# The causal mask moves from a matmul to the operation that finds each head's maximum

## The reference

```
h   = layernorm(x)
q   = rope(h @ Wq)        # 32 heads of 64
k   = rope(h @ Wk)        # 8 key-value heads of 64, each shared by 4 query heads
v   = h @ Wv
s   = q @ k.T / sqrt(64)
s   = where(key <= query, s, -3.4e38)         # the causal mask
out = softmax(s) @ v
x   = x + out @ Wo
x   = x + ffn(layernorm(x))   # activations rounded to int8 per token, int8 weights
```

## Time and profile before

| | before |
|---|---|
| median of 3 runs | 802.25 us (799.59 to 802.53) |
| profiled execution | span 803.9 us (the page gives no other time of it) |
| TensorE, weight loads | 761.0 us (95%), 640.0 us (80%) busy |
| VectorE, ScalarE, GpSimd | 629.2 us (78%), 628.4 us (78%), 569.1 us (71%) busy |
| granted TensorE clock, mean | 0.987 of full speed |
| mask matmuls (L720) | 352, mean 254 ns |
| maxima (L1367) | 352 reduces, mean 635 ns |
| exponentials (L1028) | 512, mean 530 ns, and 512 accumulator reads |

### The profile page before, as it was taken

How to read it: one execution, slowest core, us unless ns; L and a number is a source line. 1 busy time by engine, 2 the same in 40 slices (tenths; PEclk the granted TensorE clock), 3 DMA queues, 4 the chain that set the end, 5 groups by cost and what they waited for, 6 DMA issues and landing times.

```text
span 803.9 us, 23412 instructions
## 1 busy us (share of the span) xinstructions
PE 761.0 (95%) x8230; PEld 640.0 (80%) x8230; DVE 629.2 (78%) x1392; ACT 628.4 (78%) x1734; POOL 569.1 (71%) x524
## 2 busy tenths in 40 slices
PE   5799999999999999999999999999999999999993
PEld 3578888888888887788888888888888888888782
DVE  5757787777787887777788888887788877877887
ACT  4577888787877887787788778887788778888873
POOL 3467868787768786877786887778686787686402
PEclk9899999999999999999999999999999999999996
DMA  8255544554555554455554455455454555454300
GB/s 267 56 119 114 130 119 118 132 141 111 127 121 108 118 118 93 117 117 119 115 121 108 113 128 120 104 128 122 106 117 107 122 116 126 93 116 97 87 8 27
DMA packets 56994, 90.99 MB, mean 113 GB/s; under 512 B 12592, under 2 KB 19248, under 8 KB 56880
## 3 DMA queue, kind: packets, MB, share of 16 engines
q1 hardware_dynamic: 53808, 79.02, 43.0%
q0 software_dynamic: 3072, 10.49, 5.0%
HBM read 16.06 MB, written 2.10 MB: 23 GB/s over the span
## 4 chain that ended last, share of the span: by engine, by line
PE 71%; DVE 6%; ACT 6%; SPq 5%; issue 5%; DMA 5%; POOL 2%; ACTq 0%; POOLq 0%; DVEq 0%
PE x_bank L621 21%; PE t_bank L733 14%; PE o_bank L749 11%; PE s_bank L717 9%; PE s_bank L718 8%; DMA qT<-wv 4%; PE s_bank L720 3%; PE t_bank L621 3%; PE ot_bank L800 2%; ACT prob L1028 2%; SPq L303 2%; DVE probT L1356 2%; SPq L337 1%; SPq L341 1%; DVE o_norm L1391 1%
## 5 line engine op out<-in xcount | busy, mean ns | idle before, releaser
L1028 ACT ACTIVATE prob<-s_bank,neg_max 128x384 f32<-128x384 f32 (+3 forms) x512 | 266.1, 530 | 64.9 <-DVE neg_max L1367 64.8
L1367 DVE TENSOR_REDUCE neg_max<-s_bank 128x1 f32<-128x384 f32 (+3 forms) x352 | 215.6, 635 | 60.3 <-PE s_bank L720 57.3
L1356 DVE SCALAR_TENSOR_TENSOR probT<-t_bank,probT 128x512 f16<-128x512 f32 x320 | 215.4, 681 | 29.6 <-ACT probT L1040 28.8
L1040 ACT ACTIVATE probT<-t_bank 128x512 f16<-128x512 f32 x320 | 189.0, 600 | 43.8 <-PE t_bank L733 38.8
L733 PE MATMUL t_bank<-ident,prob 128*128 128x128 f32 x1280 | 199.1, 278 | 5.1 <-DVE probT L1356 1.7
L717 PE MATMUL s_bank<-kT,qT 128*128 128x384 f32 (+3 forms) x512 | 178.3, 363 | 6.7 <-DMA qT<-wv 4.2
L491 POOL TENSOR_TENSOR wv<-raw,wv 128x512 fp32r<-128x512 f32 x62 | 79.4, 1280 | 134.2 <-ACT wv L989 134.2
L718 PE MATMUL s_bank<-kT,qT 128*128 128x384 f32 (+3 forms) x512 | 157.1, 322 | 0.0
L733 PEld LDWEIGHTS t_bank<-ident,prob 128*128 128x128 f32 x1280 | 137.6, 141 | 15.0 <-issue 7.5
L749 PE MATMUL o_bank<-value,probT 128*128 128x64 f16 x3840 | 138.5, 193 | 0.0
L749 PEld LDWEIGHTS o_bank<-value,probT 128*128 128x128 f16 x3840 | 131.4, 98 | 6.1
(11 more groups left out here) (123 smaller groups left out, 946.8 us busy)
## 6 DMA issues: line engine op xcount, KB each, us to landing
qT<-wv SPq DMA_DIRECT2D x248, 128.0 KB, 2.4
swp<-raw SPq DMA_DIRECT2D x320, 64.0 KB, 2.0
kT<-key_pair SPq DMA_DIRECT2D x128, 128.0 KB, 2.4
wg_raw<-in_w_group POOLq DMA_DIRECT2D x16, 384.0 KB, 4.9
wg_raw<-in_w_group POOLq DMA_DIRECT2D x16, 256.0 KB, 4.3
resid<-in_x SPq DMA_DIRECT2D x4, 512.0 KB, 7.5
out<-resid SPq DMA_DIRECT2D x16, 128.0 KB, 2.1
wo_stage<-in_w_out SPq DMA_DIRECT2D x4, 256.0 KB, 3.5
```

Source lines behind the costliest of these rows:

```text
L1028: nc.scalar.activation(prob[:, slot:slot + blocks, h, :], s_bank[G % SCORE_BANKS][:, at * n:(at + 1) * n].rearrange("p (k n) -> p k n", n= ...
L1040: nc.scalar.activation(turned_half[B % TURNED][HI], t_bank[B % TURN_BANKS][:, :], ACT.Copy, scale=PROB_SCALE).then_inc(probT_hi, 1)
L1356: nc.vector.scalar_tensor_tensor(out=turned_half[B % TURNED][LO], in0=t_bank[B % TURN_BANKS][:, :], scalar=PROB_SCALE, in1=turned_half[B % ...
L1367: nc.vector.tensor_reduce(neg_max[:, s % 2, u:u + len(heads)], s_bank[G % SCORE_BANKS][:, 0:len(heads) * n].rearrange("p (h n) -> p h n", ...
```

## The change

The mask matmul goes, and the last score matmul signals instead. In place of one reduce per group VectorE runs one fused operation per head: it adds a row of a wider mask (`mask_row`, 512 columns, zero but for the last 128) to the scores, multiplies by -1, writes the result back in place, and keeps its minimum, which is the negated maximum. The exponential then takes the negated scores with scale -1. The tile for the mask grows to four times its columns, and other small buffers share places (`ones` lies in a part of `prob` that is written later, `stats` is used in turn, `in_inv` shares with `root_t`).

```diff
+UNBOUNDED = 3.4e38
-        mask = sb("mask", [P, P], bf16)
+        mask_row = sb("mask_row", [P, SEQ], bf16)
-        in_inv = sb("in_inv", [P, TOK_TILES], f32)
+        in_inv = root_t
+        ones = prob[:, 3, 3, :].bitcast(bf16)[:, 0:P]
...
-            nc.gpsimd.memset(mask[:, :], 0.0).then_inc(const_zeroed, 1)
+            nc.gpsimd.memset(mask_row[:, :], 0.0).then_inc(const_zeroed, 1)
...
                     nc.tensor.matmul(bank, q, kT[s % 2][:, HI, 0:n], start=(at == 0), stop=False, skip_group_check=True)
-                    nc.tensor.matmul(bank, q, kT[s % 2][:, LO, 0:n], start=False, stop=False, skip_group_check=True)
-                diagonals = s_bank[G % SCORE_BANKS][:, 0:len(heads) * n].rearrange("p (h n) -> p h n", n=n)[:, :, i * P:n]
-                nc.tensor.matmul(diagonals, ident_b[:, :], mask[:, :].unsqueeze(1).broadcast_to([P, len(heads), P]),
-                                 start=False, stop=True, skip_group_check=True).then_inc(scores_done, 1)
+                    last = nc.tensor.matmul(bank, q, kT[s % 2][:, LO, 0:n], start=False, stop=True, skip_group_check=True)
+                last.then_inc(scores_done, 1)
...
-                                     ACT.Exp, bias=neg_max[:, s % 2, u:u + 1],
+                                     ACT.Exp, bias=neg_max[:, s % 2, u:u + 1], scale=-1.0,
...
-                nc.vector.tensor_reduce(neg_max[:, s % 2, u:u + len(heads)],
-                                        s_bank[G % SCORE_BANKS][:, 0:len(heads) * n].rearrange("p (h n) -> p h n", n=n),
-                                        AX.X, ALU.max, negate=True).then_inc(max_done, 1)
+                if G == 0:
+                    dve.wait_ge(const_ready, 6)
+                for at in range(len(heads)):
+                    bank = s_bank[G % SCORE_BANKS][:, at * n:(at + 1) * n]
+                    last = nc.vector.tensor_tensor_reduce(bank, bank, mask_row[:, SEQ - n:SEQ], -1.0, UNBOUNDED, ALU.add, ALU.min,
+                                                          neg_max[:, s % 2, u + at:u + at + 1])
+                last.then_inc(max_done, 1)
```

More of the change, by code:

```diff
@@ L47 @@
 LN_STEPS = 5
+STATS = 2 * Q_TILES
 def attention_ffn_kernel(nc: bass.Bass, x: bass.AP, w_group: bass.AP, w_value: bass.AP, w_out: bass.AP,
@@ L76, in attention_ffn_kernel @@
         ident_b = sb("ident_b", [P, P], bf16)
-        mask = sb("mask", [P, P], bf16)
+        mask_row = sb("mask_row", [P, SEQ], bf16)
         zero = sb("zero", [P, 1], f32)
         magic = sb("magic", [P, 2], f32)
-        ones = sb("ones", [P, P], bf16)
         pow_rows = sb("pow_rows", [P, KV_HEADS], f32)
@@ L112, in attention_ffn_kernel @@
         oT = sb("oT", [P, 2, 2 * P], f32r)
-        stats = sb("stats", [P, TOK_TILES, 6], f32)
+        stats = sb("stats", [P, STATS, 6], f32)
         mean_var = sb("mean_var", [P, TOK_TILES, 2], f32)
@@ L397, in _ @@
             load_group_weights(0)
-            nc.gpsimd.memset(ones[:, :], 1.0).then_inc(const_ready, 1)
+            nc.gpsimd.memset(ones, 1.0).then_inc(const_ready, 1)
             nc.gpsimd.memset(ident[:, :], 0.0).then_inc(const_zeroed, 1)
             nc.gpsimd.memset(ident_b[:, :], 0.0).then_inc(const_zeroed, 1)
-            nc.gpsimd.memset(mask[:, :], 0.0).then_inc(const_zeroed, 1)
+            nc.gpsimd.memset(mask_row[:, :], 0.0).then_inc(const_zeroed, 1)
             nc.gpsimd.memset(zero[:, :], 0.0).then_inc(const_zeroed, 1)
@@ L408, in _ @@
                                         pattern=[[-1, P]], channel_multiplier=1).then_inc(const_ready, 1)
-            nc.gpsimd.affine_select(out=mask[:, :], in_=mask[:, :], compare_op=ALU.is_ge, fill=MASKED, base=0,
+            nc.gpsimd.affine_select(out=mask_row[:, SEQ - P:SEQ], in_=mask_row[:, SEQ - P:SEQ], compare_op=ALU.is_ge, fill=MASKED, base=0,
                                     pattern=[[-1, P]], channel_multiplier=1).then_inc(const_ready, 1)
@@ L677, in _ @@
             for k in range(K_TILES):
-                last = nc.tensor.matmul(o_bank[:, :], ones[:, :], wv_abs[k], start=(k == 0), stop=(k == K_TILES - 1))
+                last = nc.tensor.matmul(o_bank[:, :], ones, wv_abs[k], start=(k == 0), stop=(k == K_TILES - 1))
             last.then_inc(wv_summed, 1)
@@ L1207, in done_statistics @@
                 dve.wait_ge(resid_added, part_no(s, f % Q_TILES) + 1)
-                nc.vector.bn_stats(stats[:, f, :], resid[:, t, :]).then_inc(stats_done, 1)
+                nc.vector.bn_stats(stats[:, f % STATS, :], resid[:, t, :]).then_inc(stats_done, 1)
             def tile_statistics(t):
-                nc.vector.bn_stats(stats[:, t, :], resid[:, t, :]).then_inc(stats_done, 1)
+                nc.vector.bn_stats(stats[:, t % STATS, :], resid[:, t, :]).then_inc(stats_done, 1)
             def aggregate(first_tile, end_tile, done):
@@ L1216, in aggregate @@
                     dve.wait_ge(stats_done, done + end_tile)
-                    nc.vector.bn_aggr(mean_var[:, t, :], stats[:, t, :]).then_inc(aggr_done, 1)
+                    nc.vector.bn_aggr(mean_var[:, t, :], stats[:, t % STATS, :]).then_inc(aggr_done, 1)
                 dve.wait_ge(aggr_done, done + end_tile)
```

## The result

The changed kernel takes 806.93 us (median of 20 runs, 803.99 to 809.68) against 803.82 for the kernel before on the same chips (20 runs, 799.59 to 807.53). The ratio is 1.0033, 95% interval 1.0019 to 1.0047: slower by a third of a per cent, where 798 and faster were forecast. As a ratio it lies within the 0.5% that I had called no change (806.93 itself is above the 806.3 named there, which was reckoned from 802.25), and inside the range.

What follows compares the result with a forecast made beforehand. TensorE was taken to set the time, with VectorE's maxima on or near the path in each step's first third. Mean step shift -0.19 us, -6 over 31 steps, 2 given back: 802.25 - 4 = 798; own range 784 to 807, range 775 to 830.

Steps and rivals of the forecast that it cites:

- e: VectorE's maxima: cost of a fused operation beyond a reduce of as many elements; taken as 0.08 us, bounds 0 and 0.21.
- T1: First transpose of query tile 3, awaiting its exponentials; forecast shift at 0.08: +0.03 us in odd steps, -0.78 in even.
- 2 us given back for the feed-forward: Twelve steps with feed-forward VectorE operations between the maxima: an estimated 0.2 us lost in each, 2 us.
- The odd step, walked: VectorE's order followed through a step without key projection: the step's end shifts by -0.89, +0.07 or +1.89 us.
- the step: Odd step's end, set by the later of TensorE's T2 and VectorE's normalisation; +0.07 us odd, -0.45 even at 0.08.
- T2: Transpose behind the last exponential of query tile 2; forecast shift at 0.08: -0.09 us in odd steps, -0.61 in even.
- TensorE's saving: Mask matmuls leaving TensorE's chain: 1.3 us a step, 0.85 before T1; 41 us if TensorE waited for nothing.
- TensorE waits more for ScalarE ahead of T1: Sign to look for in odd steps: some 0.8 us more of TensorE waiting for ScalarE.
- VectorE's busy time: Whole kernel: forecast to go from 629 to some 680 us, with maxima taking 7.8 us a step.
- The first: Rival on VectorE's fused operation: e up to 0.03, TensorE keeps most of its saving, 771 to 785 us; chance 0.22.
- The second: Rival: e of 0.12 or more, VectorE's maxima set each step's first two thirds, 815 us at 0.12; chance 0.28.
- The third: Rival: the change does not free TensorE, even steps keep little, time stays at 802 us; chance 0.05.

Runs made afterwards that it cites:

- e3: Kernel before, with one copy without exchange in place of the four copies that swap halves for the queries' rotation; 799.97 us, ratio 0.9954.
- e4: Changed kernel, with one copy without exchange in place of the four copies that swap halves; 796.26 us, ratio 0.9918.
- e6: Changed kernel, with the second half of the next step's queries placed ahead of the swap of halves on SyncE's queue; 800.62 us, ratio 0.9944.
- e7: Kernel before, with the second half of the next step's queries placed ahead of the swap of halves on SyncE's queue; 799.66 us, ratio 0.9941.
- e1: Kernel before without its mask matmuls, maxima by the old reduction, nothing masked; 786.15 us against 803.77, ratio 0.9797.
- e9: Kernel before without its mask matmuls and with the next queries placed ahead of the swap on SyncE's queue; 785.64 us against 803.21, ratio 0.9771.
- e2: Changed kernel with the mask matmul put back, adding zeros, so VectorE does the new operations and TensorE all its former work; 818.69 us, ratio 1.0204.
- e5: Changed kernel with each step's first score group masked by matmul and reduced once as before, groups 1 to 10 new; 799.57 us against 805.42, ratio 0.9927.
- e10: Changed kernel with only group 0 new, groups 1 to 10 masked by matmul and reduced as before; 806.20 us against 803.21, ratio 1.0036.

## Why the prediction was wrong, point by point

**The books.** A to D gain 0.03 + 0.11 + 0.15 - 0.13 = 0.16 us a step, 5.0 us. E loses 5.5 by the runs e3, e4, e6 and e7, uncertain by some 3 (the two traces of the table, one execution each, show 0.10 a step, some 3 us). The side edits cost some 1.0, uncertain by 1.2. That makes +1.5, against a measured +2.6 by the ratio (1.5 to 3.8). The 5.5 holds the measured difference itself, so this sum proves less than the one with the queue relieved, where E is alike: e4 should lie 5.0 - 1.0 = 4.0 us under e3, and lies 2.9 under it by the ratios, 3.7 by the medians. What is left, about 1 us, is within those intervals and not settled. The start is a candidate: the first scores of a program come at 52.3 us in the trace of before and 53.6 in that of after, but with 50.7 to 55.5 over all the traces, and e1 and e9, which hold none of the side edits, have them at 53.1 and 54.9. Nothing here ties it to the change.

**The price e of the fused form** was too high. The read starts 616, 483, 360 and 248 ns after its stream for 512, 384, 256 and 128 elements (medians of the starts in the trace), and the next operation, where it has nothing to wait for, starts with the read. Against a reduce's 608 and 465, and my 0.34 and 0.20 for the narrow ones, e is 0.01, 0.02, 0.02 and 0.05, not 0.08. The two rows are what the Trainium skill, "VectorE: DVE Perf Modes", section "Two Vector instructions with no wait between them", says of an operation with an accumulator output, which it counts as two instructions. The trace agrees on the two rows, but the 143 ns of the read lie beside the next operation and delay only the release behind the last one of a group. I had let that rule exclude e near 0, and by the row it doesn't.

**What I said would follow from so small an e, faster, did not.** I had written that under 0.04 the forecast fails on the fast side, 771 to 785. My own walk at e = 0.024, between its columns for 0 and 0.08, gives -0.42 for T1 in odd and -0.83 in even steps, -0.62 in the mean, and -0.76 for the whole step; 31 of these, with 2 us given back for the feed-forward as before, from 802.25: 781. Measured: T1 -0.14 (A and B), the step -0.06. So the e that I had put too high was worth some 17 us of the forecast, what the walk left out some 26, and the one error hid most of the other: that 798 came near and the range held is luck.

**The step that failed: "The odd step, walked".** I followed group 0's four operations down VectorE's own list ("end at 401.04 + 4e (before: 401.08)") and on to T1, but not over to ScalarE, whose exponentials of group 0 give the bank to the scores of group 3. The length was about right, 1.19 at e = 0.08 against 1.10 measured (397.67 to 398.77); what hangs on it was missed. This is 0.40 of the 0.43 that TensorE sheds in A, taken where e1 and after differ by nothing but VectorE's part and the side edits: 3.44 and 3.84. e2, e5 and e10 bear it out from three sides. In the kernel before, the slack was 0.2 us and no row showed a wait at these scores, so no view of waits could have named it.

**The second failure: the step's end.** I let "the step" end with TensorE or VectorE's normalisation and added the shifts up over 31 steps. But the next step begins with the scores of group 0, which need queries that come by way of ScalarE, SyncE's queue and DMAs. E is 2.0 where TensorE sets it; the mean in before was 2.23, with 14 of 30 steps over 2.1, and in after 20 of 30. So TensorE's gain, once it had got so far, was partly waited away. The chain had 5% on that queue and 5% on DMAs, and I did not use them. D gives back 0.13 as well; that is there in e1 too (0.09), without the fused operations. Perhaps a shorter way to T2 doesn't bring the copies of ScalarE and VectorE that free the turn banks behind it forward as much; that is not shown, and no run tested it.

**What was right.** T1 to T2 came out near what was walked, -0.15 against -0.19 at the measured e; whether by the chain that was walked is not shown (e1 has -0.21 without the new operations). TensorE's saving of 0.22 for group 0 and some 0.1 each for groups 1 and 2 is in A of e1, 0.43. TensorE waits more for ScalarE ahead of T1, by 20.6 us in front of the first score matmuls' weight loads (7.0 to 27.6 over the whole program), and VectorE's share of the chain rose above 6%, to 12%. Group 0's first operation starts right behind its last score matmul (397.67). VectorE's busy time rose, by 27 and not by 51 us, as e is smaller: the spacings make 4 x (0.616 + 0.483 + 0.360 + 0.248) = 6.8 us of maxima a step, not 7.8.

**The rivals.** The first had its condition met and not its result. The second, slower by VectorE's pace everywhere, had the right sign by the wrong mechanism: e is under its 0.09, and e2's loss sits at the step's head alone. The third is refuted by e1.

## What to carry to other kernels

When work moves to an engine that is not the bottleneck, follow each longer operation to every buffer that it holds, over the engines behind it, until the buffer's next writer: slack of 0.2 us there shows as no wait in the profile before, and a chain 0.41 us longer costs 0.2 or eats 0.4 of a gain. A group that is released by one signal should not be split into several operations where its buffer is the next to come back; mixed treatment (the old way for that group, the new for the rest) was worth more than either pure version. And a loop's saving counts only as far as the step's start, which may hang on DMA queues, moves with it: measure with that queue relieved in both kernels before judging a change.

## What the runs showed of the hardware

- A VectorE operation with an accumulator output that follows another starts before the first one's row ends: spacings of 616, 483, 360 and 248 ns for streams of 703, 578, 446 and 324. The Trainium skill, "VectorE: DVE Perf Modes", section "The DRAIN you can't avoid", lets the next operation wait until the pipe is empty, and refers to the section "Two Vector instructions with no wait between them" for those that aren't held; by these spacings, 76 to 95 ns shorter than the rows, these weren't.
- Adding a second input and a write back into PSUM made the stream of 512 elements no more than 8 ns slower in spacing than a reduce (616 against 608).
- The exchange of two neighbours on one DMA queue was worth 0.6% to the kernel before (e7), though TensorE was busy 95% of the time.
